# Perceiver on one core: the long cross attention by pairs of heads, scores from 64 ranks per head, low-rank queries in column halves, weights rounded in 15 jobs

## The reference, cut to what matters

```python
q_hk = (hidden_q @ Wq.T).reshape(B, S, H, K)              # S 256, H 16, K 128
q_big = rope(einsum('bshk,hkq->bshq', q_hk, w_kc_q))      # q 384
kv_r = rope(kv_c)                                         # L 4096 x 128
q_r = einsum('bshq,hqr->bhsr', q_big, W_qr)               # r 64
k_r = einsum('bld,hdr->bhlr', kv_r, W_kr)
attn = softmax(einsum('bhsr,bhlr->bhsl', q_r, k_r))
ctx_c = einsum('bhsl,bld->bhsd', attn, kv_r)
out = einsum('bhsd,hkd->bhsk', ctx_c, w_kc_kv).reshape(B, S, H * K) @ Wo.T
# last MLP: weights rounded per row to 127 steps of scale = max|w| / 127
```

## Time and profile before

| | us |
|---|---|
| median of 3 runs | 1131.75 (1131.22 to 1132.66) |
| profiled execution, its own time | 1130.86 |
| span of its instructions | 1129.2 |
| TensorE busy | 1066.1 (94%) |
| VectorE busy | 760.1 (67%) |
| ScalarE busy | 544.7 (48%) |
| GpSimd busy | 334.2 (30%) |
| mean granted TensorE clock | 0.986 |

### The profile page before, as it was taken

How to read it: one execution, slowest core, us unless ns; L and a number is a source line. 1 busy time by engine, 2 the same in 40 slices (tenths; PEclk the granted TensorE clock), 3 DMA queues, 4 the chain that set the end, 5 groups by cost and what they waited for, 6 DMA issues and landing times.

```text
span 1129.2 us, 19389 instructions
## 1 busy us (share of the span) xinstructions
PE 1066.1 (94%) x6663; PEld 862.3 (76%) x6663; DVE 760.1 (67%) x1314; ACT 544.7 (48%) x1075; POOL 334.2 (30%) x232
## 2 busy tenths in 40 slices
PE   7989999999998998999999999999999999899995
PEld 5545889999976665888888888888898889677742
DVE  3656466556636666878888878888877887464545
ACT  3344354454423221666556566666566667343422
POOL 6810243444333000023333213333311333404411
PEclk9999899999999999999999999999999999999998
DMA  9450167655503334112111232212222211223010
GB/s 281 94 222 1 42 225 256 219 201 216 182 25 118 109 103 163 59 30 41 32 35 17 40 40 40 35 35 29 23 40 40 40 31 40 24 76 154 1 61 19
DMA packets 70510, 97.07 MB, mean 86 GB/s; under 512 B 35361, under 2 KB 52929, under 8 KB 69314
## 3 DMA queue, kind: packets, MB, share of 16 engines
q1 hardware_dynamic: 70466, 96.50, 30.2%
HBM read 91.58 MB, written 4.90 MB: 85 GB/s over the span
## 4 chain that ended last, share of the span: by engine, by line
PE 73%; DVE 17%; issue 5%; ACT 3%; DMA 1%; POOL 1%; DVEq 0%; SPq 0%; ACTq 0%; POOLq 0%
PE PS L1362 11%; PE PS L1471 11%; PE PS L1491 10%; PE PS L1481 7%; PE PS L1381 5%; DVE qsL L1024 3%; DVE pL L1050 3%; DVE scores L1030 3%; PE PS L1420 2%; PE PS L1439 2%; PE PS L1429 2%; PE PS L1210 2%; PE PS L1549 2%; PE PS L1508 1%; PE PS L1632 1%
## 5 line engine op out<-in xcount | busy, mean ns | idle before, releaser
L1030 DVE TENSOR_SCALAR_CACHE_REDUCE scores<-PS 128x512 f32<-128x512 f32 x256 | 173.9, 689 | 87.8 <-PE PS L1471 87.0
L750 ACT ACTIVATE scores<-scores,nmX 128x512 f32<-128x512 f32 x256 | 181.9, 714 | 52.8 <-DVE nmX L1034 52.4
L768 ACT ACTIVATE pH<-PS 128x1024 fp32r<-128x1024 f32 x128 | 131.0, 1023 | 152.9 <-PE PS L1481 152.9
L550 POOL TENSOR_TENSOR wrow<-wrow,winv 88x1024 f32<-88x1024 f32 x16 | 30.3, 1892 | 466.8 <-DVE winv L1070 466.8
L1050 DVE TENSOR_TENSOR pL<-PS,pH 128x1024 fp32r<-128x1024 f32 x128 | 156.2, 1220 | 7.5 <-ACT pH L768 7.5
L1481 PE MATMUL PS<-ident,scores 128*128 128x128 f32 x1024 | 136.4, 274 | 17.9 <-ACT scores L750 16.1
L1481 PEld LDWEIGHTS PS<-ident,scores 128*128 128x128 f32 x1024 | 115.9, 141 | 44.5 <-issue 34.0
L1491 PE MATMUL PS<-pH,kvH 128*128 128x256 f32 x512 | 146.5, 286 | 0.3
L1491 PE MATMUL PS<-pH,kvL 128*128 128x256 f32 x512 | 144.7, 283 | 0.0
L1491 PE MATMUL PS<-pL,kvH 128*128 128x256 f32 x512 | 144.4, 282 | 0.0
L1471 PE MATMUL PS<-kvTH,qsH 128*128 128x512 f32 x256 | 111.2, 434 | 2.0 <-DVE qsL L1024 1.5
(11 more groups left out here) (305 smaller groups left out, 2298.0 us busy)
## 6 DMA issues: line engine op xcount, KB each, us to landing
rawG<-in_wg SPq DMA_DIRECT2D x16, 768.0 KB, 5.7
rawU<-in_wu SPq DMA_DIRECT2D x16, 768.0 KB, 7.2
rawD<-in_wd SPq DMA_DIRECT2D x16, 768.0 KB, 6.3
wrow<-in_w SPq DMA_DIRECT2D x16, 352.0 KB
win<-in_win SPq DMA_DIRECT2D x1, 4640.0 KB, 17.5
wblk<-blocks SPq DMA_DIRECT2D x4, 1056.0 KB, 8.1
wb<-w_rows SPq DMA_DIRECT2D x32, 128.0 KB, 3.3
wqX<-in_wqX SPq DMA_DIRECT2D x16, 256.0 KB, 2.6
```

Of the source, the lines that this page charges most:

```text
L750: act.activation(at, at, ACT.Exp, bias=nmX[:, b, q:q + 1], accum_out=csum[:, b, q, c:c + 1]).then_inc(exp_done, 1)
L768: act.activation(pH[:, c % 2], PS[:, 2 + 2 * (c % 2):4 + 2 * (c % 2), :].rearrange("p k (h t) -> p (k h) t", t=T), ACT.Copy).then_inc(pH_r ...
L1030: dve.tensor_scalar(sp_[:, q, c * CH:(c + 1) * CH], PS[:, q, :], 1.0, None, ALU.mult, ALU.max, accum_out=cmax[:, q, c:c + 1]).then_inc(sX_ ...
```

## The change

The attention goes by 8 pairs of heads (`XP`), with 16 slots (`SLOTS`) per pair: slot j is chunk j // 2 of head j % 2.

- `p4` is gone. `p3` does two heads at once, head 0 into PSUM partitions 0 to 63, head 1 into 64 to 127 (12 records), and `qr` (128 = 2 x 64 ranks, by pair) is kept.
- `keys(p, c)`: the weights of both heads' keys (128 x 128) times the context chunk, three matmuls into bank 7; ScalarE's `high_keys` and VectorE's `low_keys` split them into `keyH`, `keyL`, which lie over the memory of `kvr`. ScalarE therefore waits for `kvL_ready` before its first `high_keys`, and the wait stands ahead of its first copy `qh`.
- `scores(p, s)`: slot s is chunk s // 2, query half s % 2; both heads on row groups 0 to 63 and 64 to 127, in banks 0 and 1, three matmuls each. A slot waits for both evacuations of the slot before (`sX_out`, 2 per slot).
- The prologue makes both heads' scores of pair 0, 16 slots.
- Exponentials run two slots ahead. Low parts of queries and key weights go to GpSimd, two pairs ahead.
- `values` and four `head_out` of the pair before stand in slots 2, 4, 6, 8, 10.
- Rounding: 15 jobs (`JOBS`), 11 of 256 rows of w1 (128 x 1024, in `xn`'s memory), 4 of 128 rows of w2 (128 x 1408); two per pair, maxima in slots 0 and 2 and in 12 and 14. Stored in plain order, so the last MLP reads and writes contiguously.
- `win` is loaded in two parts, the last one behind the last rounding store. Loops are written out.

```diff
+            def p3(m):
+                pe.wait_ge(qb_ready, 2 * m + 2)
+                for j in range(QT):
+                    for h in range(2):
+                        mm = pe.matmul(PS[XR * h:XR * h + XR, 6, (m % 2) * T:(m % 2 + 1) * T], wqr[:, 2 * (m % 2) + h, j, :], qb[:, 2 * (m % 2) + h, j, :], ...)
-            def p4(n, i, b):
-                pe.matmul(PS[:, 7, 0:T], wkr[:, b, :], qr[:], start=True, stop=True).then_inc(p4_done, 1)
+            def keys(p, c):
+                for j, (w, v) in enumerate(((wkrH, kvTH), (wkrH, kvTL), (wkrL, kvTH))):
+                    mm = pe.matmul(PS[:, 7, :], w[:, p % 2, :], v[:, c * CH:(c + 1) * CH], start=(j == 0), stop=(j == 2))
+            for n in range(XH):
+                if n + 1 < XH:
+                    p1(n + 1, (n + 1) // 2, (n + 1) % 2)
+                if n % 2 and n >= 3:
+                    p3((n - 3) // 2)
+                p2(n, n // 2, n % 2)
+                if n % 2:
+                    wait(pe, keyL_ready, n // 2)
+                    keys(0, n // 2)
+            p3(XP - 1)
+            def scores(p, s):
+                c, q = s // 2, s % 2
+                wait(pe, sX_out, 2 * (p * SLOTS + s))
+                for j, (w, v) in enumerate(((qsH, keyH), (qsH, keyL), (qsL, keyH))):
+                    for h in range(2):
+                        rank = slice(XR * h, XR * h + XR)
+                        mm = pe.matmul(PS[:, h, :], w[rank, p % 2, q * P:(q + 1) * P], v[rank, c * CH:(c + 1) * CH], ...)
+            for s in range(SLOTS):
+                scores(0, s)
+                if s == 1:
+                    keys(1, 0)
+            for p in range(XP):
+                more = p + 1 < XP
+                for j in range(SLOTS):
+                    turn(p, j)
+                    if j and more:
+                        scores(p + 1, j - 1)
+                    if p and j == 2:
+                        values(p - 1)
+                    if p and j in (4, 6, 8, 10):
+                        head_out(p - 1, (j - 4) // 4, (j - 4) // 2 % 2, 7)
+                    if j % 2 and j + 1 < SLOTS and more:
+                        keys(p + 1, (j + 1) // 2)
+                    if j:
+                        weigh(p, j - 1)
+                    if j == SLOTS - 2 and p + 2 < XP:
+                        keys(p + 2, 0)
+                    if j == SLOTS - 1 and more:
+                        scores(p + 1, SLOTS - 1)
+                weigh(p, SLOTS - 1)
 (VectorE)
+            for p in range(XP):
+                for j in range(SLOTS):
+                    if j and p + 1 < XP:
+                        scores_out(p + 1, j - 1)
+                    if p and j in (4, 6, 8, 10):
+                        add_out(p - 1, (j - 4) // 4, (j - 4) // 2 % 2, 7)
+                    if j % 2 and j + 1 < SLOTS and p + 1 < XP:
+                        low_keys(p + 1, (j + 1) // 2)
+                    dve.wait_ge(pH_ready, SLOTS * p + j + 1)
+                    dve.tensor_tensor(pL[:, j % 2], ...)
+                    if j == SLOTS - 2 and p + 2 < XP:
+                        low_keys(p + 2, 0)
+                    if p + 1 < XP and j in (0, 2):
+                        row_max(2 * p + 1, j // 2)
+                    if p + 1 < XP and j in (12, 14):
+                        row_max(2 * p + 2, (j - 12) // 2)
+                    if j == SLOTS - 1 and p + 1 < XP:
+                        scores_out(p + 1, SLOTS - 1)
 (SP)
+            for p in range(XP):
+                sp.wait_ge(wint_ready, 2 * p + 1)
+                if p + 1 < XP:
+                    load_rows(2 * p + 1)
+                store_rows(2 * p)
+                if p:
+                    sp.wait_ge(oX_ps, 4 * p)
+                    load_out(p)
+                if p + 1 < XP:
+                    sp.wait_ge(wint_ready, 2 * p + 2)
+                    load_rows(2 * p + 2)
+                    store_rows(2 * p + 1)
 (last MLP)
-                dve.tensor_tensor(gs[:, n % 2].rearrange("p (t r) -> p t r", t=GT), PS[:, 2 + 2 * (n % 2), 0:FC].rearrange("p (t r) -> p t r", t=GT), scale1(c), ALU.mult)
+                dve.tensor_tensor(gs[:, n % 2], PS[:, 2 + 2 * (n % 2), 0:FC], scale1(c), ALU.mult)
```

More of the change, by code:

```diff
@@ L561, in _ @@
+            step(pool.memset(rounding[:], ROUND))
+            for p in range(2):
+                low_parts(p)
+            pool.wait_ge(qr_ready, XP)
+            for n in range(JOBS):
+                round_rows(n)
+                if n % 2 == 0 and n // 2 + 2 < XP:
+                    low_parts(n // 2 + 2)
             rstd(4)
@@ new lines, in _ @@
+            act.wait_ge(kvL_ready, 1)
+            for n in range(XH):
+                act.wait_ge(p1_done, n + 1)
+                wait(act, p2_done, n - 1)
+                act.activation(qh[:, n % 2], PS[:, n % 2, 0:T], ACT.Copy).then_inc(qh_ready, 1)
+                if n % 2 and n >= 5:
+                    ranks_out((n - 5) // 2)
+                    if (n - 5) // 2 < 2:
+                        high_query((n - 5) // 2)
+                if n % 2 == 0 and n:
+                    high_keys(0, n // 2 - 1)
@@ L1484, in weigh @@
-            def weigh(n, c):
-                pe.wait_ge(pL_ready, n * NCH + (c + 1))
-                if c == 0:
-                    wait(pe, cT_ready, n)
-                for j in range(4):
-                    for k, (w, v) in enumerate(((kvH, pH), (kvH, pL), (kvL, pH))):
-                        mm = pe.matmul(PS[:, 6, 0:T], w[:, 4 * c + j, :], v[:, c % 2, j, :],
-                                       start=(c == 0 and j == 0 and k == 0), stop=(c == NCH - 1 and j == 3 and k == 2))
-                mm.then_inc(v_done, 1)
@@ L1510, in pe_scores @@
-            def pe_scores(n, i, b):
-                last = isinstance(n, int) and n + 1 >= XH
-                for c in range(NCH):
-                    if c:
-                        turn(n, c)
-                    if not last:
-                        scores(n + 1, 1 - b, c)
-                    if c:
-                        weigh(n, c - 1)
-                    if not (isinstance(n, int) and n == 0):
-                        if c == 1:
-                            values(n - 1, 1 - b, i + b)
-                        if c in (4, 7):
-                            head_out(n - 1, 1 - b, c // 7)
-                if not last:
-                    turn(n + 1, 0)
-                weigh(n, NCH - 1)
@@ new lines, in turn @@
+            def turn(p, j):
+                h, c = j % 2, j // 2
+                wait(pe, pL_ready, SLOTS * p + j - 1)
+                for q in range(NT):
+                    pe.wait_ge(exp_done, 2 * SLOTS * p + (2 * q + h + 1 if c == 0 else 2 * j + q + 1))
+                    for m in range(4):
+                        at = (m % 2) * T + q * P
+                        mm = pe.transpose(PS[:, 2 + 2 * (j % 2) + m // 2, at:at + P], sp_[:, h, q, (4 * c + m) * P:(4 * c + m + 1) * P], ident[:])
+                mm.then_inc(t_done, 1)
@@ new lines, in weigh @@
+            def weigh(p, j):
+                h, c = j % 2, j // 2
+                pe.wait_ge(pL_ready, SLOTS * p + j + 1)
+                if c == 0:
+                    wait(pe, cT_ready, p)
+                for m in range(4):
+                    for k, (w, v) in enumerate(((kvH, pH), (kvH, pL), (kvL, pH))):
+                        mm = pe.matmul(PS[:, 6, h * T:(h + 1) * T], w[:, 4 * c + m, :], v[:, j % 2, m, :],
+                                       start=(j == 0 and m == 0 and k == 0), stop=(c == NCH - 1 and m == 3 and k == 2), skip_group_check=True)
+                mm.then_inc(v_done, 1)
@@ L1539, in _ @@
+            values(XP - 1)
+            pe.wait_ge(vX_ready, XP)
+            for h in range(2):
+                for q in range(NT):
+                    head_out(XP - 1, h, q, 2 * h + q)
+            stay_awake(14, 7)
             for t in range(NT):
```

509 lines of the change are left out of this document (249 added, 260 removed).

## The result

The change makes the kernel slower by 0.9%: 1141.82 us median of 5 runs (1137.38 to 1145.95) against 1131.35 (1130.09 to 1132.66) on the same chip, a ratio of 1.0089, 95% interval 1.0059 to 1.0119. The forecast was 1140.

The account below looks back on a forecast made before the run. TensorE, busy for 94% of 1129.2 us, was taken as the bound. Low-rank phase -13, prologue +28.5, pairs -5, additions +1.6 and MLP -3.5 gave +8.6 on the median 1131.75: about 1140 us, range 1114 to 1160.

Parts of the forecast that it names:

- pair 0: First pair of heads, without values or outputs: 60.0 of work, 1.2 and 6.8 of waits, 68 us in all.
- Score slots: Attention scores on 64-row groups: 0.70 plus 0.40 per visit, 1.10 us per slot instead of 1.39; 4.7 saved per pair.
- Rival 1: Visits to the row halves cost nothing in the pairs: 45 less, VectorE's queue taking back some 7, 1102 us; 20%.
- Pair period: Middle pair of heads: 64.3 of TensorE work plus waits of 1.2 and 1.5, 67.0 us.
- (a): Pair boundary: slot 14's rounding maximum on VectorE delays slot 15's weighted sum by about 1.2 us; bounds 0 to 2.
- (b): Odd rounding job's rows land late for slot 0's maximum: TensorE loses 1.5 us per pair, 6.8 in the first.
- The last pair: Last pair of heads, with neither scores nor keys: 41.1 us of work, 43 with the chain in it.
- Prologue: First pair's scores, matmuls and evacuations without overlap, 2.75 per slot: 46 us against 17.6, 28.5 lost; bounds 39 to 51.
- Low-rank phase: Products ahead of the scores: 8.4 per two heads against 10.96, later start; 13 us gained, bounds 8 to 18.
- Additions and MLP: Stage end: four serial additions, 1.6 us lost; final gated MLP with contiguous reads and writes, 3.5 gained (0 to 7).
- Rival 2: VectorE's queue becomes the bound in odd slots of the pairs: 39 more, 1175 us; 10%.
- Rounding rows: Rounding stores and next block's input weights in the last pair's shadow: no cost, some 5 us if last store late.

Follow-up runs that it names:

- e1: Changed kernel with each slot's scores as three matmuls on all 128 rows, no row halves, scores wrong: 1110.04 us, ratio 0.9816 to the kernel before.
- e11: e9 with each slot's scores as three full-array matmuls, both heads summed, no row halves: 1051.96 us, ratio 0.9300 to the kernel before.
- e2: Changed kernel with only head 0's three score matmuls per slot, head 1's dropped: 1145.92 us, ratio 1.0129 to the kernel before.
- e9: Changed kernel with e4, e5 and e6 together, even jobs' maxima in slots 10 and 12, next rows loaded before output weights: 1087.50 us, ratio 0.9606.
- e5: Changed kernel with the odd rounding jobs' maxima in slots 4 and 6 instead of 0 and 2: 1124.37 us, ratio 0.9932 to the kernel before.
- e7: Changed kernel with three unused bf16 matmuls of 512 columns in every prologue slot: 1135.32 us, ratio 1.0032 to the kernel before.
- e4: Changed kernel with odd prologue slots in two other banks, waiting for evacuations only two slots later: 1116.70 us, ratio 0.9881 to the kernel before.
- e12: e10 with GpSimd making the context's low part in 8 pieces instead of one instruction: 1083.77 us, ratio 0.9575 to the kernel before.
- e6: Changed kernel with ScalarE's wait for the context's low part moved behind the first queries: 1141.63 us, ratio 1.0088 to the kernel before.
- e10: e9 with low and rounded parts of the first two pairs' key weights made ahead of the context's: 1086.19 us, ratio 0.9593 to the kernel before.
- e3: Changed kernel with the same six score matmuls per slot, each on all 128 rows: 1174.06 us, ratio 1.0388 to the kernel before.

## Why the prediction was right, step by step

The forecast of 1140 and the sign came from a large loss that the diff hardly shows (the prologue) against several small gains, and every term had the right sign. Part of the closeness is luck. The start of the low-rank phase 1.4 earlier, which the change didn't cause, hides half of what the prologue was short by, and inside the pairs pair 0 was 2.4 above its forecast, the six middle pairs together 3.6 below and the last 0.7 above.

- **Score slots: 1.10 forecast, 1.08 measured.** The price of a visit was taken from another stage's shape, 0.40; here it is 0.38. e1 and e11 remove it, e2 shows the overlap. So the rewrite gains 16 x (1.39 - 1.08) = 5.0 per pair, and the keys cost 5.5: the finding that the pairs stay as long as they were (66.5 before, 66.4 after) is shown: TensorE's work rose by 0.9 (63.4 to 64.3) and its waits fell from 3.1 to 2.1. Rival 1 is refuted by the first block of 0.89 in the chain. Having no visits at all is worth 31.8 in the changed kernel (e1) and 35.5 in the evened one (e11): rival 1 had 45, and 38 with what VectorE's queue takes back. Its size was near the mark; it was wrong in that the visits are not free. The 1.1 of the chain, six records in a block, has to be read as 0.89 and the 0.19 behind it.
- **Pair period: 67.0 forecast, 66.4 measured.** TensorE's sum was right (64.3 against 63.96 busy, and e9's period). The waits (a) and (b) were put at 1.2 and 1.5. (b) is 1.7, which e5 removes; what e5 leaves above e9's 64.30 is 64.74 - 64.30 = 0.4, and that is all that (a) can be. So (a) is the term that made the pair's forecast too long. Pair 0, from the prologue's end to the same point of pair 1, lasted 70.4 against 68: the rows came 8.2 late for the maximum, where I had 6.8 lost. The last pair, to the last weighted sum, took 43.7 against 43.
- **Prologue: 46 forecast, 49 measured.** The mechanism was right (both banks in one slot, no overlap), the size was off in one term: I took 2.75 per slot, midway between full and half clock. The clock was at half for 38.6 of the 49 us, so the slot was 3.1, near the 3.0 that I had worked out for that case. e7 prices the clock at 8.7, e4 both it and the missing overlap at 25.
- **Low-rank phase: -13 forecast, -12.2 measured.** GpSimd released the first copy 11.2 after the phase had begun, and the second product started 0.1 from where I had it once the 1.4 are allowed for. Doubles of heads took 8.39 for 8.4. The term that was too small is the end: rotation of the last head and its p3 took 3.84 + 2.35 = 6.2 (the row at 421.80 above; p3 is 1.45 in mid-stage), where I had 4.5 (3.5 and 1.0); in this p3 the granted clock was 0.61. The start was 0.6 better than put. The chain of waits (start, us, what), against the earlier trace rows:

```profile
344.65 8.82 POOL kvL L553
...
354.02 2.90 PE PS L1479 x6
...
364.00 1.73 PE PS L1470 x8
365.73 1.45 PE PS L1490 x12
367.17 1.49 PE PS L1479 x6
368.67 0.70 PE PS L1499 x3
369.37 1.73 PE PS L1470 x8
371.09 1.29 PE PS L1479 x6
```

- **Additions and MLP**: +1.6 and -3.5 forecast, +1.6 and -3.6 measured. The MLP row (chain) that answers to the earlier trace rows, 0.88 before:

```profile
1115.21 0.53 DVE gs L1243
```

- **Rounding rows**: no cost at the last pair, as forecast.

Rival 2 (VectorE as the bound) did not come: 50.8 busy of 66.4, and away from the pair's boundary the chain runs through TensorE alone. It is near, though: in e11, at 59.1 per pair, its products stand in the chain.

Open: why pairs 1 and 2 lengthened in e7, why the sixth pair is 1 to 5 us longer than the others in several executions (not in e9 to e12), and what decides whether the granted clock is already at half when the prologue starts. One execution of each kernel is profiled, and runs of the changed kernel spread over 8.6 us, so that gains below 2 are read from the traces and not from the times.

## What to carry to other kernels

A rewrite that halves a product's steps can leave a steady stage as it was: count the entries to and exits from the other array shape, per visit, before the columns saved. When two jobs begin to share what they used to alternate in (here two banks in one slot), look at the stage that has no other work to hide it: that is where the loss was, and two more banks repaid 25 us. After moving a wait, look at what is queued behind the awaited instruction, and on the engine that is shut out while it runs: e6 uncovered the key weights, e10 the wait for qb that e12 then shortened. And when an edit moves the instruction from which a stage is measured, take a mark that it leaves alone: in e10 a gain of 2.4 shrank to 1.4 by that.

## What the runs showed of the hardware

- A block of six 512-column matmuls on two row groups takes 0.89 between full-array blocks, 0.70 of it columns; the next full-array block is 0.19 to 0.20 longer. With one group idle the block is just as long (e2).
- Slots with 0.98 of matmuls in 2.4 were followed by the fall to 1.2 GHz. In e3, with 1.67 in 3.1, the clock was at 1.2 GHz in the first scores, back at 2.4 GHz by 428 and stayed there to the end of the prologue. In e2, e5 and e6, with prologue slots that wait for the same evacuations, it was at 1.2 GHz from 425 to 471.
- A small store of scales took 9.53 us to land (e4), issued behind a load and four larger stores, more than the 4.0 of the 512 KB load. VectorE waited for 2.2 of it.
- One GpSimd subtraction of 8.9 us stretched a VectorE subtraction with two SBUF inputs from 0.96 to 5.19; in 8 pieces it stretched it to 1.26 and 1.77, at a cost of 2.4 on GpSimd.
